# Gather passes of a graph kernel: one semaphore and one relay for eight gathers, and step addresses as two 16-bit words

## The chip, the cores and the metric

The kernel is one program on one core of a Trainium2 chip. The metric is the device time of one execution in microseconds (us), as the median of the runs; runs differ by some tenths of a per cent.

## The reference, cut to what matters

Four graph layers over N = 50000 nodes with 64 features and 50000 edges, each followed by a residual and mostly a layer norm. What matters here is the aggregation, which every layer has in some form: fetch a row for every edge by one index, and add it to the row of another index.

```python
edge_index = jnp.stack([src, dst])       # src random, dst sorted, 50000 * u**2
# layer 0
msgs = x[col] * norm[:, None]
out = jax.ops.segment_sum(msgs, row, num_segments=n)
# layer 1
transformed = xw[r, src]
out = jax.ops.segment_sum(transformed, dst, num_segments=num_node)
# layer 3, twice
return jax.ops.segment_sum(msg, dst, num_segments=n) + b
```

## The kernel before, in words

The program runs stage after stage, with a barrier between any two. It sorts the edges by source and by destination (each time 392 indirect DMAs write them to a list, L599), and then does four *stair passes* (`stair_pass`: e0, e1, e3, e4), an edge network (`mlp_pass`, which has a gather loop, two stair loops and semaphores of its own), and dense node passes in between (`node_pass`). Only the stair passes and the table that they read are touched.

**A stair pass.** The sorted edges lie in T = 392 tiles of 128; the nodes in 392 buckets of 128. Because edges are sorted, all pairs (tile, bucket) that share an edge form a stair, with STEPS = 784 steps, and each step either takes the next tile or the next bucket. A step is one product on TensorE: the one-hot matrix of the tile's destinations, times the 128 x 64 messages of the tile, added into the bucket's 64 columns of a ring in PSUM. Steps are done in GROUPS = 49 groups of GS = 16. The engines split the work so:

- GpSimd (POOL) issues one indirect DMA for each tile (L925), 392 in a pass, which gathers 128 rows into `msgs`, a ring of HELD = 128 tiles in SBUF. Gather i adds 16 to semaphore `slot{i % 8}` when it has landed, and gather i waits for gather i - 8 (L924). From tile 128 on, each batch of SLOTS = 8 gathers waits also for `s_room` (L922), that is, until the tiles that it overwrites have been used.
- SyncE (SP) relays. For each batch it waits for the group of TensorE that last uses the old tiles and adds 1 to `s_room` (L937 to L941), and then for each of the batch's eight tiles waits for its slot semaphore and adds 1 to `s_ready` (L943, L944). `s_ready` so counts the landed tiles in order.
- VectorE (DVE) makes the group's 16 one-hots with one instruction (L977), loads two words from `gates`, how many tiles and how many banks the group needs (L980, L981), waits until `s_ready` and `s_free` have reached them (L982, L983), and adds 1 to `s_go` (L985).
- TensorE (PE) loads the group's 16 step words from `table` into registers (L1046), waits for `s_go` (L1050), and does 16 matmuls (L1058). Both addresses of a step, the tile's column in `msgs` and the bucket's in the ring, lie packed in one 32-bit word, so each matmul has two register instructions ahead of it: REGISTER_ALU (in the trace ALU_OP) and ISA (in the trace FUSED_REGOPS). In the trace each f32 matmul is two MATMUL with two LDWEIGHTS.
- ScalarE (ACT) copies each full bank of the ring to `stage`, scaled in e3 and e4, and stores it (L1092 to L1131), and fills the bank with its starting rows.

What sets the order is therefore written out by hand; there is no scheduler. `Sorter.dve_table` (L438 to L495) makes `table`, `gates` and other tables on one partition; it runs twice, for the sources ahead of e0, and for the destinations inside e0, behind group 35. `mlp_pass` reads `table` of the sources as well and masks it for its own rings (L1367).

Of the kernel before, what the change touches and what calls it, by code (L numbers as in the profile page):

```python
# [10 lines left out]
I32 = mybir.dt.int32  # L11
# [234 lines left out]
class Sorter:  # L246
# [190 lines left out]
    def dve_table(self, dve):  # L437
# [23 lines left out]
        if "halves" in order:  # L461
# [5 lines left out]
            buckets = order["table"][:, :]  # L467
# [18 lines left out]
        nc.vector.tensor_scalar(gates[:, :, 1:2], rows_c[:, :, GS - 1:GS], 1.0, None, ALU.add)  # L486
        self.step(dve, nc.vector.tensor_copy(order["table"][:, :], self.steps_i[:, :]))
        self.step(dve, nc.vector.tensor_scalar(order["table"][:, :], order["table"][:, :], HELD - 1, None,
                                               ALU.bitwise_and))
        self.step(dve, nc.vector.tensor_scalar(order["table"][:, :], order["table"][:, :], 6, None,  # L490
                                               ALU.logical_shift_left))
        self.step(dve, nc.vector.tensor_scalar(self.within[:, :], self.within[:, :], 22, None,
                                               ALU.logical_shift_left))
        nc.vector.tensor_tensor(order["table"][:, :], self.within[:, :], order["table"][:, :], ALU.bitwise_or
                                ).then_inc(self.sem("steps"), 1)  # L495
# [338 lines left out]
def stair_pass(nc, label, K, order, column, source, sums, fresh=None, sort=None, extra=None, turned=None,  # L834
# [8 lines left out]
    with ExitStack() as ctx:  # L843
# [19 lines left out]
        s_land = K["slots_dma"]  # L863
        before = K["landed"]()
# [52 lines left out]
        def _(pool):  # L917
            if fresh is not None:
                pool.wait_ge(s_index, 1)
            for i in range(T):  # L920
                if i >= HELD and i % SLOTS == 0:
                    pool.wait_ge(s_room, (i - HELD) // SLOTS + 1)  # L922
                if i >= SLOTS:
                    pool.wait_ge(s_land[i % SLOTS], before + 16 * (i // SLOTS))  # L924
                pool.indirect_dma_start(  # L925
                    out=msgs[:, (i % HELD) * D:(i % HELD + 1) * D], out_offset=None, in_=source,
                    in_offset=bass.IndirectOffsetOnAxis(ap=order["index"][column][:, i:i + 1], axis=0)
                ).then_inc(s_land[i % SLOTS], 16)

        @block.sync  # L930
        def _(sp):
# [3 lines left out]
            for b in range(BATCHES):  # L935
# [5 lines left out]
                for i in range(b * SLOTS, (b + 1) * SLOTS):  # L941
                    sp.wait_ge(s_land[i % SLOTS], before + 16 * (i // SLOTS + 1))
                    sp.sem_inc(s_ready, 1)  # L943
# [76 lines left out]
        def _(pe):  # L1020
# [24 lines left out]
            for g in range(GROUPS):  # L1045
                _, at = nc.values_load_multi_w_load_instructions(  # L1046
                    order["table"][0:1, g * GS:(g + 1) * GS], [mybir.EngineType.PE], min_val=0,
                    max_val=((RING * BL - 1) * D << 16) + (HELD - 1) * D,
# [1234 lines left out]
def gnn(nc, x, src, dst, rel, ew, W, eW1, eb1, eW2, eb2, nW1, nb1, nW2, nb2, W1, b1, W2, b2, We, be, out):  # L2283
# [24 lines left out]
    with ExitStack() as ctx:  # L2308
        def sb(name, shape, dt=F32):
            return ctx.enter_context(nc.sbuf_tensor(name, shape, dt))  # L2310
# [120 lines left out]
```

## Time and profile before

| what | us |
|---|---|
| median of 3 runs | 5162.78 |
| lowest and highest of them | 5155.84, 5186.35 |
| span of the profiled execution | 6462.1 |
| stair passes in it (first gather to last matmul) | about 685, 657, 660, 660 |

The profile is of one execution with the hardware profiler on. The page gives its span and no further time of its own; the runs are timed without the profiler. The span is 1299 us, or 25%, above the median of the runs. Times of single instructions and the order of events are read from the profile; the length of a stretch has to be read with that difference in mind.

### The profile page before, as it was taken

How to read it: one execution, taken by the hardware profiler on the slowest of the kernel's cores; microseconds unless marked ns; L12 is line 12 of the kernel's file. 1: busy time of each engine (PE TensorE's matmuls, PEld its weight loads, DVE VectorE, ACT ScalarE, POOL GpSimd, SP SyncE). 2: the span in 40 equal slices, each digit the busy share in tenths (PEclk: the TensorE clock that was granted, in tenths of full speed). 3: DMA queues.
4: the chain of work that ended last, by engine and by line, in shares of the span. 5: the costliest groups of instructions: out<-in, count | busy, mean ns of one | idle time of the engine just before them, and what ended most of it. 6: DMA issues, size and time to landing. Idle time of an engine off the chain costs nothing. (4 is left out here: it accounts for less than half of the span.)

```text
span 6462.1 us, 74448 instructions
## 1 busy us (share of the span) xinstructions
PE 3919.6 (61%) x19983; PEld 3086.7 (48%) x19983; DVE 2177.2 (34%) x4653; ACT 1422.3 (22%) x3080; POOL 2886.1 (45%) x2799
## 2 busy tenths in 40 slices
PE   3333451668656742667466759888952669626697
PEld 2122121667422322666265646776732668426586
DVE  7444790324645620124311102343530112102134
ACT  0000000001333420112200126443420223302135
POOL 2555406663566766661555540000146660366602
PEclk8555575555666765555555569999975555755569
DMA  3000131111445641223734436554631222412235
GB/s 99 2 2 2 47 113 33 43 42 42 155 175 202 234 153 38 66 70 138 264 99 101 107 116 202 181 180 181 227 113 35 69 69 84 145 36 69 69 106 177
DMA packets 354959, 692.13 MB, mean 107 GB/s; under 512 B 183337, under 2 KB 185254, under 8 KB 339130
## 3 DMA queue, kind: packets, MB, share of 16 engines
q1 hardware_dynamic: 148381, 491.73, 21.7%
q10 hardware_dynamic: 118428, 130.12, 6.0%
q0 software_dynamic: 87808, 66.01, 5.8%
q8 instruction: 182, 2.98, 0.2%
q14 instruction: 160, 1.30, 0.1%
HBM read 350.87 MB, written 349.58 MB: 108 GB/s over the span
## 5 line engine op out<-in xcount | busy, mean ns | idle before, releaser
L1058 PE MATMUL e_ring<-e_msgs,e_hot 128*128 x6272 | 1419.4, 413 | 1091.3 <-issue 1082.7
L1058 PEld LDWEIGHTS e_ring<-e_msgs,e_hot 128*128 128x128 f32 x6272 | 1385.0, 328 | 1127.4 <-issue 1125.9
L925 POOL DMA_INDIRECT e_msgs<-y,index_D x784 | 741.4, 946 | 640.9 <-POOLq L77 261.1
L977 DVE TENSOR_TENSOR e_hot<-e_nodes,keys_D 128x2048 f32<-128x2048 f32 x147 | 336.9, 2292 | 1596.9 <-remote 872.0
L599 POOL DMA_INDIRECT list_D<-d_place,d_target x392 | 456.2, 1164 | 326.6 <-DVEq L553 210.5
L925 POOL DMA_INDIRECT e_msgs<-y,index_S x392 | 396.8, 1012 | 387.7 <-DVE index_S L963 198.3
L599 POOL DMA_INDIRECT list_S<-s_place,s_target x392 | 390.6, 996 | 362.8 <-DVEq L553 247.5
L1241 POOL DMA_INDIRECT m_far<-x,index_S x392 | 390.9, 997 | 347.9 <-DMA pairs_by_edge<-m_far 221.4
L1410 PE MATMUL m_ring<-m_region,m_hot 128*128 x1568 | 375.9, 426 | 215.7 <-issue 213.3
L925 POOL DMA_INDIRECT e_msgs<-x_by_relation,index_D x392 | 374.0, 954 | 210.4 <-issue 112.8
L1410 PEld LDWEIGHTS m_ring<-m_region,m_hot 128*128 128x128 f32 x1568 | 348.1, 328 | 244.3 <-issue 242.2
L2086 POOL TENSOR_TENSOR n_sq<-n_cent 128x1792 f32<-128x1792 f32 x14 | 44.4, 3175 | 837.0 <-DVE n_cent L1981 837.0
L1096 ACT ACTIVATE e_stage<-e_ring,dinv 128x64 f32<-128x64 f32 x784 | 171.6, 330 | 1078.5 <-DMA pairs_by_edge<-m_stage 475.6
L804 PE MATMUL s_p_deg<-s_hot_low,s_hot_high 128*128 128x392 f16 x784 | 256.0, 473 | 160.0 <-DVE s_hot_low L709 152.0
L1745 PE MATMUL d_p_w<-wall,d_xt 64*128 64x512 f32 x784 | 300.8, 808 | 80.9 <-DVE d_stage L1704 55.6
L1092 ACT COPY e_stage<-e_ring 128x512 f32<-128x512 f32 x98 | 57.4, 586 | 1211.1 <-remote 903.4
L2099 POOL TENSOR_TENSOR n_out<-n_cent,n_rstd 128x1792 f32<-128x1792 f32 x28 | 89.4, 3192 | 453.0 <-DVE n_rstd L1991 453.0
L1467 PE MATMUL m_ring<-m_region,m_hot 128*128 x1568 | 227.7, 303 | 59.6 <-issue 52.0
L1467 PEld LDWEIGHTS m_ring<-m_region,m_hot 128*128 128x128 f32 x1568 | 214.6, 190 | 72.7 <-issue 68.6
L1345 DVE TENSOR_SCALAR m_hot<-m_keyrow,slots 128x2048 f32<-128x2048 f16 x49 | 63.3, 1292 | 515.0 <-remote 280.1
L977 DVE TENSOR_TENSOR e_hot<-e_nodes,keys_S 128x2048 f32<-128x2048 f32 x49 | 112.2, 2290 | 341.9 <-remote 242.1
L522 DVE SCALAR_TENSOR_TENSOR s_scratch<-s_p_k,low_src,before 128x128 bf16<-128x128 f32 x392 | 113.6, 344 | 334.6 <-remote 303.4
(368 smaller groups left out, 5846.1 us busy)
## 6 DMA issues: line engine op xcount, KB each, us to landing
x_by_relation<-d_stage SPq DMA_DIRECT2D x98, 1024.0 KB
agg<-e_stage ACTq DMA_DIRECT2D x196, 256.0 KB
n_in<-agg SPq DMA_DIRECT2D x42, 896.0 KB, 5.6
x<-n_out SPq DMA_DIRECT2D x28, 896.0 KB, 3.6
m_keyrow<-keys_by_step SPq DMA_DIRECT2D x49, 512.0 KB
m_region<-pairs_by_edge SPq DMA_DIRECT2D x49, 512.0 KB
messages<-m_region SPq DMA_DIRECT2D x98, 256.0 KB
m_region<-messages SPq DMA_DIRECT2D x49, 512.0 KB, 4.1
```

The costliest lines, as they stand in the source:

```text
L522: op = self.nc.vector.scalar_tensor_tensor(out=self.scratch[:, h, j, :], in0=of[:, j, :], scalar=self.low[:, t:t + 1], in1=self.K["before" ...
L599: pool.indirect_dma_start(out=self.listing, out_offset=bass.IndirectOffsetOnAxis(ap=self.target[:, t:t + 1], axis=0), in_=self.place[:, t, ...
L804: mm = nc.tensor.matmul(p_deg[m // QUADS][:, 0:T], hot_high[m % 2][:, j, :], hot_low[m % 2][:, j, :], start=q == 0 and j == 0, stop=q == Q ...
L925: pool.indirect_dma_start(out=msgs[:, (i % HELD) * D:(i % HELD + 1) * D], out_offset=None, in_=source, in_offset=bass.IndirectOffsetOnAxis ...
L977: nc.vector.tensor_tensor(hot[g % 2][:, :, :], bc(nodes[:, 0:P].unsqueeze(1), [P, GS, P]), bc(order["keys"][:, g * GS:(g + 1) * GS].unsque ...
L1058: mm = nc.tensor.matmul(ring[:, bass.ds(bucket, D)], hot[g % 2][:, k, :], msgs[:, bass.ds(tile, D)], start=False, stop=False, skip_group_c ...
L1096: nc.scalar.activation(stage[r][:, k * D:(k + 1) * D], ring[:, at:at + D], ACT.Identity, scale=scale[:, m * BL + k:m * BL + k + 1]).then_i ...
L1241: pool.indirect_dma_start(out=far[:, (i % AHEAD) * D:(i % AHEAD + 1) * D], out_offset=None, in_=source, in_offset=bass.IndirectOffsetOnAxi ...
L1410: mm = nc.tensor.matmul(ring[:, bass.ds(tile, D)], hot[g % HOTS][:, k, :], region[:, bass.ds(bucket, D)], start=False, stop=False, skip_gr ...
L1467: mm = nc.tensor.matmul(ring[:, bass.ds(bucket, HID)], hot[g % HOTS][:, k, :], msgs[:, bass.ds(tile, HID)], start=False, stop=False, skip_ ...
L1745: nc.tensor.matmul(p_w[m % NW][:, :], xt[w % 2][half:half + D, k // 2, :], wall[half:half + D, :], start=True, stop=True).then_inc(s_pw, 1)
L2099: nc.gpsimd.tensor_tensor(result[0][h][:, :, :], cent[h][:, :, :], bc(rstd[h][:, :].unsqueeze(2), [P, CH, D]), ALU.mult).then_inc(s_done, 1)
```

## The change

In the stair passes the eight slot semaphores give way to two, `batch0` and `batch1`. All eight gathers of batch b add to `batch{b % 2}`; POOL waits once for each batch, for batch b - 2, and SP waits once for each batch and adds 8 to `s_ready` in one go. The sorts and the edge network keep the slot semaphores.

The table `table`, one 32-bit word for a step, becomes `pairs`, two 16-bit words for a step. PE loads 32 words for a group in place of 16. Other readers of the table view the pair as the same 32-bit word as before.

```diff
@@ dve_table
-        nc.vector.tensor_scalar(gates[:, :, 1:2], rows_c[:, :, GS - 1:GS], 1.0, None, ALU.add)
-        self.step(dve, nc.vector.tensor_copy(order["table"][:, :], self.steps_i[:, :]))
-        self.step(dve, nc.vector.tensor_scalar(order["table"][:, :], order["table"][:, :], HELD - 1, None,
-                                               ALU.bitwise_and))
-        self.step(dve, nc.vector.tensor_scalar(order["table"][:, :], order["table"][:, :], 6, None,
+        self.step(dve, nc.vector.tensor_scalar(gates[:, :, 1:2], rows_c[:, :, GS - 1:GS], 1.0, None, ALU.add))
+        pairs, tile = order["pairs"][:, :, :], self.clipped
+        self.step(dve, nc.vector.tensor_copy(tile[:, :], self.steps_i[:, :]))
+        self.step(dve, nc.vector.tensor_scalar(tile[:, :], tile[:, :], HELD - 1, None, ALU.bitwise_and))
+        self.step(dve, nc.vector.tensor_scalar(tile[:, :], tile[:, :], 6, None, ALU.logical_shift_left))
+        nc.vector.tensor_copy(pairs[:, :, 0], tile[:, :]).then_inc(self.sem("pre"), 1)
+        self.n += 1
+        self.step(dve, nc.vector.tensor_scalar(self.within[:, :], self.within[:, :], 6, None,
                                                ALU.logical_shift_left))
-        self.step(dve, nc.vector.tensor_scalar(self.within[:, :], self.within[:, :], 22, None,
-                                               ALU.logical_shift_left))
-        nc.vector.tensor_tensor(order["table"][:, :], self.within[:, :], order["table"][:, :], ALU.bitwise_or
-                                ).then_inc(self.sem("steps"), 1)
+        self.step(dve, nc.vector.tensor_copy(pairs[:, :, 1], self.within[:, :]))
+        nc.vector.sem_inc(self.sem("steps"), 1)
@@ stair_pass
-        s_land = K["slots_dma"]
-        before = K["landed"]()
+        s_batch = K["batch_dma"]
+        passed = next(K["stairs"])
+        before = [16 * SLOTS * ((BATCHES + 1 - r) // 2) * passed for r in range(2)]
@@ stair_pass, gpsimd
             for i in range(T):
+                b = i // SLOTS
                 if i >= HELD and i % SLOTS == 0:
                     pool.wait_ge(s_room, (i - HELD) // SLOTS + 1)
-                if i >= SLOTS:
-                    pool.wait_ge(s_land[i % SLOTS], before + 16 * (i // SLOTS))
+                if i % SLOTS == 0 and b >= 2:
+                    pool.wait_ge(s_batch[b % 2], before[b % 2] + 16 * SLOTS * (b // 2))
                 pool.indirect_dma_start(
...
-                ).then_inc(s_land[i % SLOTS], 16)
+                    in_offset=bass.IndirectOffsetOnAxis(ap=order["index"][column][:, i:i + 1], axis=0)).then_inc(s_batch[b % 2], 16)
@@ stair_pass, sync
-                for i in range(b * SLOTS, (b + 1) * SLOTS):
-                    sp.wait_ge(s_land[i % SLOTS], before + 16 * (i // SLOTS + 1))
-                    sp.sem_inc(s_ready, 1)
+                sp.wait_ge(s_batch[b % 2], before[b % 2] + 16 * SLOTS * (b // 2 + 1))
+                sp.sem_inc(s_ready, SLOTS)
@@ stair_pass, tensor
                 _, at = nc.values_load_multi_w_load_instructions(
-                    order["table"][0:1, g * GS:(g + 1) * GS], [mybir.EngineType.PE], min_val=0,
+                    order["pairs"][0:1, g * GS:(g + 1) * GS, :].rearrange("p s c -> p (s c)"), [mybir.EngineType.PE],
...
                     tile = nc.s_assert_within(
-                        at[k] & 0xffff, 0, (HELD - 1) * D,
+                        at[2 * k], 0, (HELD - 1) * D,
...
                     bucket = nc.s_assert_within(
-                        at[k] >> 16, 0, (RING * BL - 1) * D,
+                        at[2 * k + 1], 0, (RING * BL - 1) * D,
```

On PE, at the boundary between two groups of e0, the row order before was (`hot0` and `hot1` are the one-hots of even and odd groups):

```order
L1058 REGISTER_ALU
L1058 ISA
L1058 MATMUL e0_ring<-e0_msgs,e0_hot0 128x64
L1046 TENSOR_LOAD table_S
L1058 REGISTER_ALU
L1058 ISA
L1058 MATMUL e0_ring<-e0_msgs,e0_hot1 128x64
```

and at the same place it is now

```order
L1059 ISA
L1059 MATMUL e0_ring<-e0_msgs,e0_hot0 128x64
L1047 TENSOR_LOAD pairs_S
L1059 ISA
L1059 MATMUL e0_ring<-e0_msgs,e0_hot1 128x64
```

One register instruction of two is gone from each step (784 in a pass); the load stays one instruction at the same place, now of 32 words.

On POOL, the gathers of e0 from the first one on, with the semaphores that each waits for, before:

```order
L925 DMA e0_msgs<-y0,index_S0 128x64 [waits stair_index]
L925 DMA e0_msgs<-y0,index_S0 128x64 x7
L925 DMA e0_msgs<-y0,index_S0 128x64 [waits slot0]
L925 DMA e0_msgs<-y0,index_S0 128x64 [waits slot1]
L925 DMA e0_msgs<-y0,index_S0 128x64 [waits slot2]
...
L925 DMA e0_msgs<-y0,index_S0 128x64 [waits slot0,stair_room]
L925 DMA e0_msgs<-y0,index_S0 128x64 [waits slot1]
```

and now:

```order
L928 DMA e0_msgs<-y0,index_S0 128x64 [waits stair_index]
L928 DMA e0_msgs<-y0,index_S0 128x64 x15
L928 DMA e0_msgs<-y0,index_S0 128x64 [waits batch0]
L928 DMA e0_msgs<-y0,index_S0 128x64 x7
...
L928 DMA e0_msgs<-y0,index_S0 128x64 [waits batch0,stair_room]
L928 DMA e0_msgs<-y0,index_S0 128x64 x7
```

The gathers stand in the same order; of the 384 waits for a landing in a pass, 47 are left, each on the first gather of a batch.

## Rows read from the trace of the kernel before

**Rows 1.** The page, part 2: busy tenths, granted clock and DMA in 40 slices.

```profile
PE   3333451668656742667466759888952669626697
POOL 2555406663566766661555540000146660366602
PEclk8555575555666765555555569999975555755569
```

**Rows 2.** Stretches: gathers of e3, the rest of e3, gathers of e4, its rest.

```profile
core 0: us, PE busy (x) PEld busy (x) DVE busy (x) ACT busy (x) POOL busy (x), PEclk, DMA share, GB/s
4774.00:5335.00 561.00, 268.05 (x1121) 253.09 (x1121) 81.80 (x38) 78.28 (x299) 370.74 (x392) 0.50 0.23 57
5335.00:5440.00 105.00, 97.66 (x457) 97.29 (x456) 30.82 (x14) 36.15 (x144) 0.00 (x0) 0.50 0.20 66
5580.00:6140.00 560.00, 265.56 (x1117) 251.90 (x1118) 80.49 (x37) 77.03 (x292) 370.10 (x392) 0.50 0.22 57
6140.00:6246.00 106.00, 98.65 (x460) 98.09 (x460) 32.08 (x14) 37.41 (x149) 0.58 (x1) 0.50 0.20 66
```

**Rows 3.** Timeline of e3, POOL alone: gathers without (first eight) and with a wait.

```profile
4775.45 0.95 POOL L925 DMA_INDIRECT e_msgs<-y,index_D  x1 [0.30 <-issue]
...
4782.96 0.94 POOL L925 DMA_INDIRECT e_msgs<-y,index_D  x1 [0.30 <-issue]
4784.21 0.94 POOL L925 DMA_INDIRECT e_msgs<-y,index_D  x1 [0.30 <-issue]
...
4796.72 0.95 POOL L925 DMA_INDIRECT e_msgs<-y,index_D  x1 [0.30 <-issue]
```

**Rows 4.** Line L1058 (the steps) between 4860 and 4930 us of e3.

```profile
L1058 PEldq FUSED_REGOPS  x14: 84/84/700, 4859.6 to 4925.5; - x14
L1058 PEldq ALU_OP  x13: 32/32/691, 4861.0 to 4925.4; - x13
  issue: 125.5, 50
```

**Rows 5.** The same line between 5341 and 5434 us, behind the last gather of e3.

```profile
L1058 PE MATMUL e_ring<-e_msgs,e_hot x437: 421/421/421, 5340.6 to 5433.6; 128*128 x146
L1058 PEldq FUSED_REGOPS  x213: 80/84/84, 5340.9 to 5429.7; - x107
L1058 PEldq ALU_OP  x212: 32/32/32, 5341.1 to 5429.6; - x106
```

**Rows 6.** SP's relay (L943) between 4820 and 4930 us, and in the whole trace.

```profile
L943 SPq EVENT_SEMAPHORE  x79: 649/698/1396, 4820.4 to 4929.6; - x79
...
L943 SPq EVENT_SEMAPHORE  x1568: 4/17/1397, 957.4 to 6143.1; - x196
```

**Rows 7.** DVE's one-hots between 5335 and 5434 us: groups that PE paces.

```profile
L977 DVE TENSOR_TENSOR e_hot<-e_nodes,keys_D 128x2048 f32<-128x2048 f32 x14 | 32.1, 2292 | 63.4 <-PE e_ring L1058 56.9 <-remote 6.6
```

**Rows 8.** PE's load of 16 words (L1046) between 5341 and 5434 us.

```profile
L1046 PEldq TENSOR_LOAD <-table_D x13: 1102/1387/1395, 5342.1 to 5423.2; - x13
```

**Rows 9.** The edge network's second stair loop, at the full clock: PE's steps, and two boundaries.

```profile
4300.00:4380.00 80.00, 64.56 (x449) 60.78 (x448) 30.18 (x14) 32.92 (x56) 0.00 (x0) 1.00 0.49 159
...
4304.92 4.67 PE L1467 MATMUL m_ring<-m_region,m_hot 128*128 x32 [1.15 <-issue]
...
4310.61 1.61 PE L1467 MATMUL m_ring<-m_region,m_hot 128*128 x10 [1.03 <-issue]
```

**Rows 10.** DVE's table for the destinations, in e0: the steps that change.

```profile
1541.78 0.55 DVE L487 CAST table_D<-e_steps_i 1x784 int32<-1x784 f32 x1
...
1544.14 0.96 DVE L494 TENSOR_TENSOR table_D<-e_within,table_D 1x784 int32<-1x784 int32 x1
```

**Rows 11.** Waits on a semaphore at DVE (L985) and POOL (L924).

```profile
L985 DVEq EVENT_SEMAPHORE  x196: 49/50/50, 966.4 to 6228.8; - x196
...
L924 POOLq EVENT_SEMAPHORE  x132: 17/17/17, 1108.6 to 6121.0; - x132
```

More of the change, by code:

```diff
@@ L466, in dve_table @@
             self.n += 1
-            buckets = order["table"][:, :]
+            buckets = order["pairs"][0:1, :, :].rearrange("p s c -> p (s c)").bitcast(I32)
             self.step(dve, nc.vector.tensor_scalar(buckets, self.clipped[:, :], 22, None, ALU.logical_shift_left))
@@ L920, in _ @@
             for i in range(T):
+                b = i // SLOTS
                 if i >= HELD and i % SLOTS == 0:
                     pool.wait_ge(s_room, (i - HELD) // SLOTS + 1)
-                if i >= SLOTS:
-                    pool.wait_ge(s_land[i % SLOTS], before + 16 * (i // SLOTS))
+                if i % SLOTS == 0 and b >= 2:
+                    pool.wait_ge(s_batch[b % 2], before[b % 2] + 16 * SLOTS * (b // 2))
                 pool.indirect_dma_start(
                     out=msgs[:, (i % HELD) * D:(i % HELD + 1) * D], out_offset=None, in_=source,
-                    in_offset=bass.IndirectOffsetOnAxis(ap=order["index"][column][:, i:i + 1], axis=0)
-                ).then_inc(s_land[i % SLOTS], 16)
+                    in_offset=bass.IndirectOffsetOnAxis(ap=order["index"][column][:, i:i + 1], axis=0)).then_inc(s_batch[b % 2], 16)
         @block.sync
@@ L1046, in _ @@
                 _, at = nc.values_load_multi_w_load_instructions(
-                    order["table"][0:1, g * GS:(g + 1) * GS], [mybir.EngineType.PE], min_val=0,
-                    max_val=((RING * BL - 1) * D << 16) + (HELD - 1) * D,
+                    order["pairs"][0:1, g * GS:(g + 1) * GS, :].rearrange("p s c -> p (s c)"), [mybir.EngineType.PE],
+                    min_val=0, max_val=(HELD - 1) * D,
                     skip_runtime_bounds_check_because="both parts are masked to their rings before they are stored")
@@ L1365, in _ @@
                                         ).then_inc(s_b2, 1)
-            nc.vector.tensor_scalar(table, order["table"][:, :], (WHELD - 1) << 6 | (RING * QUAD - 1) << 22, None,
+            packed = order["pairs"][0:1, :, :].rearrange("p s c -> p (s c)").bitcast(I32)
+            nc.vector.tensor_scalar(table, packed, (WHELD - 1) << 6 | (RING * QUAD - 1) << 22, None,
                                     ALU.bitwise_and).then_inc(s_table, 1)
@@ L2325, in gnn @@
         K["slots_dma"] = [semaphore(f"slot{r}") for r in range(SLOTS)]
+        K["batch_dma"] = [semaphore(f"batch{r}") for r in range(2)]
+        K["stairs"] = itertools.count()
         passes = itertools.count()
@@ L2336, in gnn @@
                       "used": sb(f"used_{n}", [1, 64], U16), "keys": sb(f"keys_{n}", [P, STEPS]),
-                      "table": sb(f"table_{n}", [1, STEPS], I32), "gates": sb(f"gates_{n}", [1, GROUPS, 2], U16), "banks": sb(f"banks_{n}", [1, 64], U16)}
+                      "pairs": sb(f"pairs_{n}", [1, STEPS, 2], U16), "gates": sb(f"gates_{n}", [1, GROUPS, 2], U16), "banks": sb(f"banks_{n}", [1, 64], U16)}
                   for n, columns in (("S", (0, 2)), ("D", (0, 2)))}
```

## Prediction

> **What bounds the kernel now.** I read four views. First the slices of the page [rows 1]: POOL is busy six or seven tenths through each stair pass and never more, PE about as much, and the clock granted to PE there is 0.5, the 1.2 GHz level. No engine is full. Second the stretches of e3 and e4 [rows 2]: 392 gathers are 561 us long though POOL is busy for only 371 of them, and then PE works alone for 99 us more. So in the profile the gathers are held up, and the pass is 660 us long. Third the timeline of POOL at the start of a pass [rows 3], where nothing holds it: a gather is 0.95 us and the next begins 0.30 us later, 1.25 us in all, 392 x 1.25 = 490 us a pass. Fourth, who holds the gathers up in the profile: PE, and PE is held by nothing of the program. Between 4860 and 4930 us a register addition, which takes 32 ns [rows 5], lasts up to 691 ns, and PE idles 125.5 us (both of its rows together) "on issue" [rows 4]; at the same time SP's semaphore steps last 698 ns against 17 in the median [rows 6]. Behind the last gather both are calm again: 457 half-matmuls take 97.6 us [rows 2], 0.2136 us each, 32 x 0.2136 = 6.84 us a group. DVE's one-hots, made one for each group that PE finishes, say the same: (32.1 + 63.4) / 14 = 6.82 [rows 7].
>
> An addition on registers touches no memory. That it takes twenty times as long while the profiler writes a record for each instruction of PE and SP I read as the profiler's own cost. It fits the other number: the span is 1299 us above the median of the runs. Taken at the gathers' pace a stair pass would be 490 us and a tail of some 10, 500 in place of 660, some 160 less in each of four passes, 640 in all; that is half of the 1299, and the edge network's first loop, which packs its steps in the same way, can hold more of it. So the picture I argue from is: without the profiler each stair pass goes at POOL's pace, 1.25 us a gather; PE needs 6.84 us a group, 49 groups or 335 us, and waits for tiles; and the end of the pass is the last gather's landing plus what PE has to do behind it.
>
> Everything below is in microseconds added to the median of the runs, 5162.8, and not to the span, since the span carries the profiler's share. The measurement tells from no change what is above about 1%, some 52 us.
>
> **The change part by part.**
>
> *POOL's waits.* In each pass 384 waits become 47: 337 fewer, 1348 in four passes. What is one worth? The first eight gathers of a pass have no such wait, and the ninth and later ones have: starts 4775.45 to 4782.96 are 7.51 us for six gathers, and 4784.21 to 4796.72 are 12.51 for ten [rows 3], 1.25 both times. A wait that is satisfied costs nothing on top. Bounds: below, nothing (a wait removed can't cost); above, the whole gap of 0.30 us that stands ahead of each gather, 1348 x 0.30 = 404 us. I take 0, since both kinds of gather stand side by side in the trace. The new wait, for batch b - 2 at the first gather of batch b, asks for a gather nine back where it was eight, so it holds nothing up; queued behind it are only the next gathers.
>
> *PE's register instruction.* It is gone 784 times a pass, 32 ns each [rows 5]: 25 us a pass of PE's sequencer. Cover: the array needs 0.427 us a step (2 x 0.2136) and the two register instructions 0.116, and in the gathers' pace PE waits for tiles anyway. Bounds 0 and 4 x 25 = 100 us less; I take 0, because behind the last gather, where PE does set the pace, matmuls follow each other with no gap while both register instructions are there [rows 2, 5].
>
> *PE's load of 32 words.* 16 words take 1.39 us [rows 8]. At the low clock they are hidden by matmuls queued earlier; in the edge network's second loop, at the full clock (1.00), a load of 16 words shows as a gap of 1.03 to 1.15 us at each group [rows 9]. If the price goes by the word, 32 take 2.78, or 1.39 more. Against that stand 16 x 0.032 = 0.51 of additions removed. Bounds: 0, and 196 groups x 0.88 = 172 us more. I take 0: the load comes ahead of the wait for `s_go`, and at the gathers' pace PE has 10 - 6.84 = 3.2 us to spare in a group of eight tiles; at the end of a pass the group's 16 steps need 16 x 0.116 + 2.78 = 4.6 us of the sequencer against 6.84 of the array.
>
> *SP's relay: the term that counts.* `s_ready` rises by eight when the eighth tile of a batch is in. A group that needs one tile of a batch now waits for all eight. In mid-pass this is a shift without a price: PE comes up to 7 x 1.25 = 8.75 us later and the ring of 128 tiles (160 us) has room for it. At the end it isn't. I counted from the reference's indices how many tiles the last groups need: by source, groups 46, 47 and 48 need 377, 385 and 392; by destination 381, 387 and 392. Before, by source, group 47 could start when tile 385 was in, seven gathers or 8.75 us ahead of the last, and was done (6.84) when the last landed; the pass ended 6.84 us behind the last landing. Now group 47 waits for the last batch, and both groups stand behind it: 13.68. That is 6.8 us more. By destination the 387 tiles were in 6.25 us ahead, so 6.84 + 0.6 before, and 13.7 now, 6.3 more; group 46 and those ahead of it are late as well by the same rounding, which brings it to about 7. Four passes: 4 x 6.8 = 27 us. Bounds: at the full clock a group is half as long and the term 14 us; if the tail were hidden, 0. I take 27, since all four passes show 0.50 [rows 1, 2], and a loop of the same steps ran for 99 us without a pause and stayed there.
>
> *DVE's table.* Removed is one `or` of 0.96, added are two copies of 0.55 [rows 10]: +0.14 us, twice; once inside e0, where DVE waits for tiles anyway, once ahead of it. The copies write 16-bit words at a stride; if that doubled them it would be 1.1 us more each time. I take 0.
>
> Sum: 0 + 0 + 0 + 27 + 0 = +27 us, 5162.8 + 27 = 5190, 0.5% slower and so within what counts as no change.
>
> **The rivals.**
>
> *A: the waits cost something that the trace hides.* The gap of 0.30 us is read with the profiler on. If a third of it were the wait, 0.10 us, 1348 would give 135 us back: 5190 - 135 = 5055. For it: the kernel's time hangs on POOL's pace over 1568 gathers. Against it: equal pitch with and without [rows 3], and where DVE and POOL do show a wait as an instruction of its own it takes 50 and 17 ns [rows 11]; at 50 the gain is 67, 5123, still no change. The Trainium skill (Advanced Engine Details and Errata, Network/Comms) gives 50 to 100 ns for reading a semaphore from a sequencer; by that, an estimate from the page's figure, 1348 waits would be 67 to 135 us and the time 5055 to 5123. The trace doesn't agree as far as the pitch goes, since nothing is added by it there.
>
> *B: the slow stretches are real.* Then the timed passes, too, are 660 and not 500 us, and PE and SP are slow at each small instruction while gathers run. One of two register instructions is gone and seven of eight relays, so about half the excess goes: 4 x 160 / 2 = 320, 5190 - 320 = 4870. Against it: there is no place left for the 1299 us between span and median.
>
> *C, slower: the load of 32 words sets the pace.* Place: the boundary of two groups on PE. Price: 0.88 us a group net, in 49 x 4 groups 172, so 5190 + 172 = 5362. It decides once the array's queue holds less than the load, that is, when PE and not POOL paces the pass and the clock is at its full level, as in rows 9. Against it: 0.50 in all four passes. Between this and my case lies one in which only the destination passes' later half is paced by PE, +27 + 74 x 0.88 = +92, 5255.
>
> *D: the tail is hidden or shorter,* because PE in the unprofiled run is at the full clock: 5163 to 5177.
>
> **How the numbers follow.** My case 0.55, D 0.13, A 0.13, B 0.07, C with its milder form 0.12. Faster by over 1% (under 5111): A and B, 0.20. Slower by over 1% (over 5214): C, 0.12. The rest, 0.68, within 1%. The range holds my case, D, the near half of A and the lower edge of C: 5085 to 5225; outside it are B, the far half of A and most of C, about 0.2.
>
> **What would show each step right or wrong.** The profiled span should fall by far more than the time: half the records of the slow stretches are gone, so e3 should be nearer 580 than 660 us with the time unmoved. If the time falls with it, B is right. The pitch of gathers should stay 1.25 us; 1.15 or less means A. The last two groups of each pass should both begin behind the relay of the last batch, where the gathers pace the pass. Loads of 32 words should last about 2.8 us with the matmuls behind the last gather still 6.84 us a group; gaps there mean C. I am wrong if the median is outside 5085 to 5225, and wrong in the reason if it is inside while the pitch of the gathers has moved.

## The result, and the profile after

The changed kernel takes 5438.64 us in the median of four runs (5433.59 to 5457.4), the kernel before 5173.91 in four runs of its own (5155.84 to 5186.35). The ratio is 1.0512, with a 95% interval of 1.0474 to 1.0551: 265 us slower. I had forecast 5190, with 5225 as the upper end of the range.

One thing has to be said of the chips. The kernel before takes 5174 us where the result was measured and 5181 on the chip of runs e8, e9 and e10 (the first kind below), and 6451, 6510 and 6515 us on three others (the second kind). Its first profile, with a span of 6462 us, looks like one of the second kind; on which chip it was taken is not on record. Every ratio of the experiments is taken on one chip, and every run says what the kernel before took there.

The page after, part 2, the same three rows as [rows 1]:

```profile
PE   4656566666784266654998797789756668666677
...
POOL 2777677735777677724777500001177740577602
PEclk9775655557888555555556899999855556655579
```

The clock of the stair passes is 0.5 as before. POOL is now seven tenths busy in a pass, where it was six; that is the chip and not the change, for in a pass of run e8, the kernel before but for one bound, POOL is busy for 370 of 489 us, here for 370 of 495. Four stretches, in the order of [rows 2]: the gathers of pass e3, its rest, the gathers of pass e4, its rest.

```profile
core 0: us, PE busy (x) PEld busy (x) DVE busy (x) ACT busy (x) POOL busy (x), PEclk, DMA share, GB/s
3951.30:4446.10 494.80, 308.10 (x1370) 296.21 (x1371) 101.00 (x45) 98.06 (x373) 369.82 (x392) 0.50 0.28 74
4446.10:4516.10 70.00, 45.75 (x208) 44.46 (x207) 11.46 (x5) 14.70 (x61) 0.91 (x1) 0.50 0.08 28
4669.40:5164.70 495.30, 308.17 (x1374) 296.78 (x1374) 101.01 (x45) 98.06 (x373) 369.81 (x392) 0.50 0.28 74
5164.70:5233.90 69.20, 45.02 (x204) 43.73 (x203) 11.46 (x5) 14.62 (x61) 0.91 (x1) 0.50 0.08 28
```

The gathers take 495 us, as I had worked out for passes without the slow stretches (490). But PE ends 70 us behind them and not 10, and it isn't busy in that time: 45.75 of 70. What it does instead is in the timeline of PE, and in the rows of its load and of its steps:

```profile
4386.27 7.08 PE L1059 MATMUL e_ring<-e_msgs,e_hot 128*128 x32 [4.14 <-issue]
4397.48 7.08 PE L1059 MATMUL e_ring<-e_msgs,e_hot 128*128 x32 [4.12 <-issue]
```

```profile
L1047 PEldq TENSOR_LOAD <-pairs_D x147: 7526/7945/8307, 1863.9 to 5218.7; - x147
L1047 PEldq TENSOR_LOAD <-pairs_S x49: 7684/7932/10655, 642.8 to 1228.5; - x49
...
L1059 PEldq FUSED_REGOPS  x3136: 55/55/65, 650.9 to 5229.4; - x196
...
  issue: 1683.6, 384
  DVEq L986: 61.8, 8
```

The load of 32 words lasts 7.9 us, where 16 words took 1.1 to 1.39 [rows 8]. It stands on PE's sequencer in the middle of a group's boundary. One of them, seen with the array at the same place:

```profile
L1047 PEldq TENSOR_LOAD <-pairs_D x2: 7938/7956/7974, 4142.8 to 4154.0; - x2
```

```profile
4154.60 3.41 PE L1059 MATMUL e_ring<-e_msgs,e_hot 128*128 x15
4162.13 7.08 PE L1059 MATMUL e_ring<-e_msgs,e_hot 128*128 x32 [4.12 <-issue]
```

The sequencer begins the load at 4154.0, when it has issued the last step of a group; the array still works off what is queued until 4158.01. So 4.0 us of the load are hidden and 4.1 us show, at each boundary. A group is 7.08 + 4.12 = 11.2 us long, 49 of them are 549, and the pass is 565 us (3951.3 to 4516.0). The gathers deliver a group's eight tiles in 10 us, so PE has become the slower one: in the 196 groups of the four passes it waits for DVE's go 8 times. The one-hots say it from DVE's side: in the 14 groups of [rows 7] 56.9 of DVE's 63.4 us of idle time ended on PE, and here, over three whole passes, 1162.6 of 1288.6.

```profile
L978 DVE TENSOR_TENSOR e_hot<-e_nodes,keys_D 128x2048 f32<-128x2048 f32 x147 | 336.9, 2292 | 1288.6 <-PE e_ring L1059 1162.6
```

SP's relay is 17 ns in all 196 cases, in [rows 6] up to 1397 (run e6, the same kernel on a chip of the second kind, has 17 ns in all 196 as well):

```profile
L944 SPq EVENT_SEMAPHORE  x196: 17/17/17, 650.8 to 5168.2; - x196
```

### The profile page after: what moved, and what is told of

It reads as the page before. It is cut to its first block and busy times, and to the rows that moved or that the text cites. A ratio compares the mean times of both kernels' runs of the same rounds, so it can differ in the third digit from the quotient of the medians.

```text
span 5455.3 us, 69944 instructions
## 1 busy us (share of the span) xinstructions
PE 3736.5 (68%) x19983; PEld 3005.4 (55%) x19983; DVE 2175.4 (40%) x4655; ACT 1416.3 (26%) x3080; POOL 2913.6 (53%) x2799
## 5 line engine op out<-in xcount | busy, mean ns | idle before, releaser
L1059 PE MATMUL e_ring<-e_msgs,e_hot 128*128 x6272 | 1388.4, 423 | 853.8 <-issue 792.0
L1059 PEld LDWEIGHTS e_ring<-e_msgs,e_hot 128*128 128x128 f32 x6272 | 1352.6, 332 | 891.6 <-issue 891.6
L978 DVE TENSOR_TENSOR e_hot<-e_nodes,keys_D 128x2048 f32<-128x2048 f32 x147 | 336.9, 2292 | 1288.6 <-PE e_ring L1059 1162.6
L600 POOL DMA_INDIRECT list_S<-s_place,s_target x392 | 407.6, 1040 | 212.7 <-issue 118.8
L1242 POOL DMA_INDIRECT m_far<-x,index_S x392 | 405.8, 1035 | 130.5 <-issue 114.0
L805 PE MATMUL s_p_deg<-s_hot_low,s_hot_high 128*128 128x392 f16 x784 | 244.1, 455 | 179.9 <-DVE s_hot_low L710 179.7
L1412 PE MATMUL m_ring<-m_region,m_hot 128*128 x1568 | 342.2, 422 | 23.3 <-DVEq L1358 20.5
L1412 PEld LDWEIGHTS m_ring<-m_region,m_hot 128*128 128x128 f32 x1568 | 337.7, 332 | 28.4 <-issue 26.6
L1747 PE MATMUL d_p_w<-wall,d_xt 64*128 64x512 f32 x784 | 227.3, 701 | 78.5 <-DVE d_stage L1706 75.9
L1469 PE MATMUL m_ring<-m_region,m_hot 128*128 x1568 | 224.4, 301 | 65.8 <-issue 55.5
L1469 PEld LDWEIGHTS m_ring<-m_region,m_hot 128*128 128x128 f32 x1568 | 213.1, 189 | 77.2 <-issue 74.8
L805 PEld LDWEIGHTS s_p_deg<-s_hot_low,s_hot_high 128*128 128x128 f16 x784 | 76.2, 119 | 305.8 <-DVE s_hot_low L710 250.0
L1774 ACT COPY d_stage<-d_p_w 128x512 f32<-128x512 f32 x294 | 160.8, 589 | 168.4 <-PE d_p_w L1747 161.1
```

The costliest lines, as they stand in the source:

```text
L600: pool.indirect_dma_start(out=self.listing, out_offset=bass.IndirectOffsetOnAxis(ap=self.target[:, t:t + 1], axis=0), in_=self.place[:, t, ...
L805: mm = nc.tensor.matmul(p_deg[m // QUADS][:, 0:T], hot_high[m % 2][:, j, :], hot_low[m % 2][:, j, :], start=q == 0 and j == 0, stop=q == Q ...
L978: nc.vector.tensor_tensor(hot[g % 2][:, :, :], bc(nodes[:, 0:P].unsqueeze(1), [P, GS, P]), bc(order["keys"][:, g * GS:(g + 1) * GS].unsque ...
L1059: mm = nc.tensor.matmul(ring[:, bass.ds(bucket, D)], hot[g % 2][:, k, :], msgs[:, bass.ds(tile, D)], start=False, stop=False, skip_group_c ...
L1242: pool.indirect_dma_start(out=far[:, (i % AHEAD) * D:(i % AHEAD + 1) * D], out_offset=None, in_=source, in_offset=bass.IndirectOffsetOnAxi ...
L1412: mm = nc.tensor.matmul(ring[:, bass.ds(tile, D)], hot[g % HOTS][:, k, :], region[:, bass.ds(bucket, D)], start=False, stop=False, skip_gr ...
```

## The experiments

The runs are called e0 to e13 after their labels; the stair passes have names of the same form, so here it is always run e3 or pass e3. Two theories. The load: words of 16 bits cost 0.25 us each on their way into a register, and the 4 us that this puts above what is hidden make nearly all of the 265. The relay: coarse steps of `s_ready` let PE begin late, and the batches cost more than the 27 us that I gave them. Beside them the question whether the slow stretches of the first profile [rows 4, 6] belong to the profiler or to the chip.

### The kernel before again, and each part alone

Run e0 is the kernel before, unchanged. Run e1 keeps the packed table and takes the semaphores and the relay of the change; run e2 keeps slots and relay and takes the pairs:

```diff
@@ e1: only this of the change
-                if i >= SLOTS:
-                    pool.wait_ge(s_land[i % SLOTS], before + 16 * (i // SLOTS))
+                if i % SLOTS == 0 and b >= 2:
+                    pool.wait_ge(s_batch[b % 2], before[b % 2] + 16 * SLOTS * (b // 2))
...
+                sp.wait_ge(s_batch[b % 2], before[b % 2] + 16 * SLOTS * (b // 2 + 1))
+                sp.sem_inc(s_ready, SLOTS)
@@ e2: only this of the change
-                    order["table"][0:1, g * GS:(g + 1) * GS], [mybir.EngineType.PE], min_val=0,
+                    order["pairs"][0:1, g * GS:(g + 1) * GS, :].rearrange("p s c -> p (s c)"), [mybir.EngineType.PE],
```

> The kernel before, unchanged, with its profile taken again. Its first profile spanned 6462 us while its runs took 5174, whereas the changed kernel's profiled span and time agree (5455 and 5457). If the slow stretches of PE and SP (1.4 us from one small instruction to the next) are the recorder's, they and a span of about 6460 should come again with a time near 5174, and the ordinary time leaves 5174 / 5439 as it is. If the first profile was a disturbed execution, the span should now be near 5174, gathers paced at 1.25 us, and each stair pass about 500 us.

> The kernel before with the two batch semaphores and one relay for eight tiles, step words still packed in 32 bits. Theory (the load of 32 words is the whole loss): 5174 plus what the coarser relay costs at the end of each pass, 0 to 27 us, so 5174 to 5201, with loads of 16 words at 1.4 us or less. Rival (the coarse relay and the batch wait hold the passes up): most of the 265 us is here, 5400 or more.

> The changed kernel with the eight slot semaphores and a relay for each tile put back; step words stay pairs of 16 bits. Theory: PE paces each pass at 11.2 us a group (a load of 8.0 us that the queued matmuls cover only in part), so the relay doesn't matter: 5430 to 5440, loads of 32 words at 8.0 us. Rival (coarse relay): back near 5174.

On this chip the kernel before takes 6450.68 us in the median. Run e0: 6454.78, with a span of 6452.7. Neither of the two cases that I had named came: the time itself is 6455. Span and time of the same execution are 2 us apart, so the long passes are in the timed runs too, and they are not the profiler's. Run e1: 6441.4, ratio 0.9999 (0.9973 to 1.0025), nothing. Run e2: 6701.87, ratio 1.0389 (1.0337 to 1.0441), 251 us. Of the two parts only the pairs cost time here, and their load is as long as in the changed kernel:

```profile
L1046 PEldq TENSOR_LOAD <-pairs_D x147: 7517/7892/8481, 2432.6 to 6468.8; - x147
```

On this chip the loss sits in another place of the pass than on the first kind. Pass e3, its gathers and its rest, in run e0 and then in run e2:

```profile
4785.80:5345.20 559.40, 269.20 (x1125) 253.82 (x1126) 82.71 (x38) 79.16 (x301) 368.88 (x391) 0.50 0.23 57
5345.20:5443.40 98.20, 96.88 (x453) 96.39 (x452) 29.79 (x13) 33.24 (x132) 0.94 (x1) 0.50 0.21 67
```

```profile
4916.20:5473.30 557.10, 253.22 (x1096) 243.32 (x1096) 82.70 (x38) 79.16 (x301) 368.85 (x391) 0.50 0.24 58
5473.30:5636.50 163.20, 106.23 (x480) 103.53 (x480) 29.79 (x13) 33.23 (x132) 0.94 (x1) 0.50 0.12 40
```

The gathers take as long as before; the 65 us are all behind the last gather, where 14 or 15 groups are still to do, at 11.1 us each in place of 6.84. On the first kind it is 49 groups that take 11.2 us where the gathers would have let them take 10. Both come to some 60 us a pass; nothing in the traces ties the two numbers to each other.

### What of the load costs: its words, their number or their width

Run e3 is the whole change, with the pairs of the destinations as 32-bit words; those of the sources stay 16-bit. (It uses an existing buffer for the edge network's blank tile, to make room, and so does run e9 below.) Run e4 loads the 32 words with two instructions of 16. Run e7 loads only the 16 words of 8 steps for a group and uses them twice. Run e5 is run e1 again and run e6 the changed kernel again, on the chip of run e4 and run e7.

```diff
@@ e3, against the changed kernel
-                      "pairs": sb(f"pairs_{n}", [1, STEPS, 2], U16)
+                      "pairs": sb(f"pairs_{n}", [1, STEPS, 2], U16 if n == "S" else I32)
@@ e4, against the changed kernel
-                    order["pairs"][0:1, g * GS:(g + 1) * GS, :].rearrange("p s c -> p (s c)"), [mybir.EngineType.PE],
+                for half in range(2):
+                    part = slice(g * GS + half * HS, g * GS + (half + 1) * HS)
+                    _, some = nc.values_load_multi_w_load_instructions(
+                        order["pairs"][0:1, part, :].rearrange("p s c -> p (s c)"), [mybir.EngineType.PE],
...
+                    at += list(some)
@@ e7, against the changed kernel
-                    order["pairs"][0:1, g * GS:(g + 1) * GS, :].rearrange("p s c -> p (s c)"), [mybir.EngineType.PE],
+                    order["pairs"][0:1, g * GS:g * GS + HS, :].rearrange("p s c -> p (s c)"), [mybir.EngineType.PE],
...
-                        at[2 * k], 0, (HELD - 1) * D,
+                        at[2 * (k % HS)], 0, (HELD - 1) * D,
```

> The changed kernel with the destinations' pairs as two 32-bit words for a step (the sources' pairs stay 16-bit; the edge network uses an old buffer for its zeros to make room). 32 words are still loaded by one instruction. Theory W (the width sets the price: 16-bit words are fetched one by one, 0.25 us each): the loads of e1, e3 and e4 fall to about 2.8 us, these passes to about 505 us, and the time by 3 x 60 us to about 5260; e0 keeps loads of 8 us. Rival C (more than 16 words is what costs): loads stay at 8 us everywhere and the time at 5439.

> The changed kernel with its load of 32 16-bit words for a group cut into two loads of 16 words. Theory W (each 16-bit word is fetched by itself, 0.25 us): two loads of 4.0 us, the time as in the changed kernel, 4 to 5% above the kernel before. Rival C (one load of more than 16 words is what costs): two loads of 1.4 us and a time within 1% of the kernel before.

> The kernel before with the batch semaphores and one relay alone, once more, to see the relay's own price. Where the kernel before takes about 5174 (gathers pace its passes) theory says 0 to 27 us more, ratio 1.000 to 1.005, with the last two groups of each pass behind the last landing; where it takes about 6450 (PE paces the passes and lags the gathers by 100 us) the relay can't show: ratio 1.000, as e1 had.

> The changed kernel, unchanged, beside the others. On a chip where the kernel before takes about 5174 it should take 5440 (ratio 1.051); on one where that takes about 6450 it should take what e2 took, 6700 (ratio 1.039), since the batch semaphores cost nothing there by e1.

> The changed kernel with only the first eight steps' words of a group loaded (16 words of 16 bits) and used again for the other eight steps, so half of the sums are of the wrong tiles and buckets; the number of matmuls and register instructions stays. Theory: a load of 4.0 us, a group of PE at about 4.0 + 3.2 = 7.2 us, below the 10 us of eight gathers; the passes go back to the gathers' pace and the time to that of the kernel before plus the relay's 0 to 27 us, where that takes 5174. Rival (something else in the pairs, not the load, costs): the time stays at the changed kernel's.

Run e3 ran on the chip of run e1: 6516.53, ratio 1.0103 (1.0057 to 1.015). One kernel has both widths in it, with the same count of 32 words:

```profile
L1047 PEldq TENSOR_LOAD <-pairs_D x147: 2127/2422/3031, 2400.8 to 6256.8; - x147
L1047 PEldq TENSOR_LOAD <-pairs_S x49: 7521/7912/10587, 956.3 to 1699.4; - x49
```

That is 0.08 us a word for 32 bits, and 0.25 for 16. The three passes with 32-bit words are back to the length of the kernel before (pass e3: 654.6 us against 657.6 in run e0), and the one pass that still has the long load, pass e0, is 762 us against 688. That is 74 us more there, and 67 more in the four passes together, where the time is 66 above the kernel before.

On the next chip the kernel before takes 6509.95. Run e4: 6777.13, ratio 1.0397 (1.0363 to 1.0432); run e6, the changed kernel: 6751.92, ratio 1.0376 (1.0341 to 1.0411). Two loads cost about as much as one, 2 x 3.8 = 7.6 us: the price hangs on the words, not on the instruction. Run e7: 6497.8, ratio 0.9992 (0.9972 to 1.0013). With half the words the load lasts 3.8 us, just under the 4.0 us of queued matmuls that hide it, and by the median the whole loss of 242 us is gone, not half of it. (In the profiles some of it stays in pass e0, 707 us in run e7 against 686 in run e5, and why is open; the other three passes agree to about 1 us.) Run e5: 6501.52, ratio 0.9986 (0.997 to 1.0003).

```profile
L1050 PEldq TENSOR_LOAD <-pairs_D x294: 3781/3796/4502, 2448.2 to 6548.8; - x147
```

```profile
L1047 PEldq TENSOR_LOAD <-pairs_D x147: 3782/3796/4703, 2379.7 to 6265.9; - x147
```

The first of the two is run e4, the second run e7.

### The relay where gathers set the pace, one register instruction, and the run-ahead

Run e10 is run e1 once more. Run e9 keeps slots, relay and the packed sources, and gives the destinations two 32-bit words for a step, with one register instruction. Run e8 is the kernel before with gathers at most 64 tiles ahead.

```diff
@@ e9, against the kernel before
-                        at[k] & 0xffff, 0, (HELD - 1) * D,
+                        tiles[k] if tiles else at[k] & 0xffff, 0, (HELD - 1) * D,
...
-                      "table": sb(f"table_{n}", [1, STEPS], I32)
+                      **({"table": sb(f"table_{n}", [1, STEPS], I32)} if n == "S" else {"pairs": sb(f"pairs_{n}", [1, STEPS, 2], I32)})
@@ e8, against the kernel before
-                if i >= HELD and i % SLOTS == 0:
-                    pool.wait_ge(s_room, (i - HELD) // SLOTS + 1)
+                if i >= WHELD and i % SLOTS == 0:
+                    pool.wait_ge(s_room, (i - WHELD) // SLOTS + 1)
```

> The batch semaphores and the one relay for eight gathers, with the packed 32-bit table as before, once more. Where the kernel before takes about 5174 us, its passes go at the gathers' pace of 1.25 us, and my term for the relay (both last groups stand behind the last batch) is 4 x 6.8 = +27 us, ratio 1.005, bounds 0 and 27. The rival is that POOL's 1348 waits do cost something (0.10 us each would be -135 us, ratio 0.974). Where the kernel before takes about 6450 to 6510 us, PE's slow groups set the pace and both theories say a ratio of 0.999 to 1.001.

> The slot semaphores of before; the destinations' addresses (three of four stair passes) as two 32-bit words with one register instruction for a step, the sources' packed as before. The load of 32 words should last 2.4 us. If the instruction saved is worth what its record says (3 x 784 x 0.032 = 75 us) and PE's sequencer sets the pace, ratio 0.985 to 0.99; if the array sets it and the load's 1.0 us more is hidden behind queued matmuls, ratio 1.000; if the load's extra is not hidden, 147 x (1.03 - 0.51) = 76 us more, ratio 1.012.

> The kernel before, with the gathers allowed only 64 tiles ahead of the steps, not 128. Theory: the slow stretches of PE and SP (register instructions of 0.7 us where they last 0.03) come from gathers that run far ahead, and end when the gathers are held; then half the run-ahead makes them shorter and the time falls, ratio below 0.98 where the kernel before takes about 6450 to 6510 us. Rival: they have nothing to do with how far ahead the gathers are; ratio 0.998 to 1.01, since PE sets the pace and 64 tiles are still 80 us of cover.

This chip is of the first kind: the kernel before takes 5181.0 us. Run e10: 5210.65, ratio 1.0057 (1.0026 to 1.0088), so the relay and its batches cost 30 us (13 to 46). Run e9: 5185.93, ratio 0.9988 (0.9955 to 1.0021): the register instruction saved on three passes, and 1.0 us more of load, show nothing either way (the interval is 17 us to each side). Run e8: 5190.54, ratio 1.0028 (0.9995 to 1.0061).

In this profile of run e8 PE has no slow stretch, so the theory of the run-ahead was not put to the test. It is the kernel before but for the run-ahead, so it also shows what [rows 2] could not: a pass at the gathers' pace. (Run e9, with 128 tiles of run-ahead, has pass e3 at 499 us; the unchanged kernel before was never profiled on such a chip.) Pass e3 in run e8, then in run e10, gathers and rest:

```profile
3804.80:4293.80 489.00, 345.19 (x1544) 333.30 (x1544) 112.43 (x50) 110.91 (x425) 369.79 (x391) 0.51 0.30 79
4293.80:4304.80 11.00, 7.08 (x32) 6.90 (x32) 0.00 (x0) 1.75 (x8) 0.95 (x1) 0.50 0.13 30
```

```profile
3838.40:4331.70 493.30, 339.53 (x1513) 327.06 (x1514) 110.19 (x49) 108.90 (x417) 368.91 (x391) 0.50 0.29 77
4331.70:4345.40 13.70, 13.66 (x65) 13.47 (x64) 2.29 (x1) 3.50 (x17) 0.94 (x1) 0.50 0.15 43
```

500.0 us against 507.0. Of the 7 only 2.7 are in the tail. The ends of PE, run e8 ahead of run e10:

```profile
4286.68 7.09 PE L1058 MATMUL e_ring<-e_msgs,e_hot 128*128 x32 [1.73 <-DVEq L985]
4297.72 7.08 PE L1058 MATMUL e_ring<-e_msgs,e_hot 128*128 x32 [3.95 <-DVEq L985]
```

```profile
4314.50 7.08 PE L1059 MATMUL e_ring<-e_msgs,e_hot 128*128 x32 [2.76 <-DVEq L986]
4324.62 20.74 PE L1059 MATMUL e_ring<-e_msgs,e_hot 128*128 x96 [3.03 <-DVEq L986]
```

In run e8 group 47 begins at 4286.68, 7.1 us ahead of the start of the last gather, and the last group waits 3.95 us for its tiles. In run e10 groups 46, 47 and 48 stand in a row of 20.74 us: 46 waited for the batch that ends with the 384th tile, and the other two queue behind it. The rest of the 7 us is in the gathers, at three places 112 gathers apart:

```profile
3976.98 0.94 POOL L927 DMA_INDIRECT e_msgs<-y,index_D  x1 [0.30 <-issue]
3978.22 0.94 POOL L927 DMA_INDIRECT e_msgs<-y,index_D  x1 [0.30 <-issue]
3981.25 0.94 POOL L927 DMA_INDIRECT e_msgs<-y,index_D  x1 [2.08 <-issue]
```

The gather after the 113th of a pass (and the 225th and the 337th) comes 3.0 us behind the one ahead of it in place of 1.25: 3 x 1.75 = 5.3 us a pass, in the passes e1, e3 and e4 of run e10 alike, and at the same gathers of the changed kernel. In run e8 and run e9, with a wait on each gather, no gather of these passes is more than 1.5 us behind the last. POOL waited for nothing that the profile shows; why it stalls is not known.

### A last look: pairs alone, half the load, the kernel before

> Slot semaphores as before, pairs of 16-bit words. Where the kernel before takes about 5174 us: the result's +265 less the relay's 30 of e10 is 235, ratio 1.045, with the loads at 7.9 us and PE setting the pace at 11.2 us a group, 49 groups in about 550 us. Rival: the two parts only hurt together (PE comes late because the relay is late), then less than 1.03. Where the kernel before takes about 6450 us: 1.039 as in e2.

> The changed kernel with only the 16 words of 8 steps loaded for a group and used twice (half of the sums go to wrong tiles and buckets). The load lasts 3.8 us, shorter than the 4.0 us by which the sequencer runs ahead of the array, so PE keeps 6.9 to 7.1 us a group, the gathers set the pace, and what stays is the relay: ratio 1.003 to 1.009. Rival: each microsecond of load counts, then half of the 235 us, ratio about 1.028.

> The kernel before. Where it takes about 5174 us, its passes e3 and e4 should be about 500 us from first gather to last matmul (392 gathers at 1.25 us and a tail of some 10), with no register instruction of 0.7 us, and the span within 10 us of the time; the 660 us of the first profile would then be that of another chip, and not the recorder's work. Rival: passes of 660 us under the profiler and a span some 1300 us above the time.

The code is that of run e2, run e7 and run e0. I had hoped for a chip of the first kind, and this one is of the second: the kernel before takes 6514.67. Run e11: 6771.46, ratio 1.0409 (1.0354 to 1.0463). Run e12: 6511.58, ratio 1.0002 (0.9979 to 1.0025). Run e13: 6502.53, with a span of 6500.5. They repeat run e2, run e7 and run e0 on another chip of the second kind and say nothing on the first kind. Pass e3 of run e13, its gathers and its rest, is that of [rows 2] again, with span and time 2 us apart:

```profile
4817.70:5381.30 563.60, 265.73 (x1114) 251.92 (x1114) 80.40 (x37) 76.82 (x292) 368.92 (x392) 0.50 0.22 57
5381.30:5482.60 101.30, 99.40 (x464) 98.86 (x463) 32.08 (x14) 35.58 (x142) 0.90 (x1) 0.50 0.20 66
```

### Where the 265 us come from

The four passes e0, e1, e3 and e4 of the changed kernel, first gather to last matmul, are 604, 565, 565 and 564 us long. In run e10, which lacks only the pairs, they are 529, 511, 507 and 507; in run e8 they are 524, 504, 500 and 500. So from run e8 to run e10 it is 25 us, from run e10 to the changed kernel 245, together 270, against 265 measured. Of the 25, some 17 are in the gathers and 7 in the tails. The split on the chips of the first kind rests on these lengths and on run e10's ratio; neither the pairs alone nor half a load was ever run on one.

## Why the prediction was wrong, point by point

**The step that failed is the term for PE's load of 32 words.** I took 0 with 172 us as the upper bound and gave the slower case a chance of 0.12; by the lengths of the passes it is 245 us. The mechanism was the one that I named in rival C, the load at the boundary of two groups. Its size was off: I priced 32 words from 16 words of another width, 2.78 us where 7.9 were measured. I knew that the words became 16-bit and still went by their number. The rows that would have warned me were in the trace of before, where single 16-bit words are loaded, on DVE and on SP:

```profile
L980 DVEq TENSOR_LOAD <-gates_D x147: 281/285/439, 2357.8 to 6226.4; - x147
```

```profile
L1332 SPq TENSOR_LOAD <-used_S x41: 248/256/472, 4109.8 to 4344.2; - x41
```

32 x 0.25 is 8.0 us. They warn, and don't prove: a load of one word can't tell a price per word from a price per load. Against it stood 16 words of 32 bits in 1.39, 0.087 a word. A bound from the nearest rows had to take both. With the 4.0 us that the trace after shows hidden (no row of before gives it), its upper end would have been 8.0 - 4.0 = 4.0 us a group on PE alone. With 49 groups of 11.1 against the gathers' 490 us a pass, that is 544 against 490, some 216 us in four passes and a time of about 5380, or about 5400 with the relay's 27. The Trainium skill (Runtime: NRT & Kernel Launch, Instruction fetch mechanics) gives about 200 ns for each register of a TENSOR_LOAD, even in bulk; by that 32 words would be, as an estimate, 6.4 us. The page speaks of loads that the runtime adds, and not of a kernel's own. The 16-bit words agree nearly, with 0.25 us; the 32-bit blocks, 0.07 to 0.09 us a word, do not.

**The condition of C was wrong too.** I wrote that it decides only "when PE and not POOL paces the pass and the clock is at its full level". At the half clock the array's queue covers 4.0 us of load, and the gathers' slack another 2.9 (10.0 - 7.08); 7.9 us are more than both, and all four passes were paced by PE at 0.50. Run e7 shows the first part from below, on the second kind of chip: behind the last gather 3.8 us of load leave a group at 7.0 us and the time where it was. (The sum beside it, 16 x 0.116 + 2.78 = 4.6 us, still held the register instruction that the change removes; without it it is 4.1. It changes nothing.)

**SP's relay: the sum was right, the working was not.** +27 was taken, and run e10 measured 30 (13 to 46). But group 47 needs 384 tiles, not 387 or 385: in run e8 it gets its go with the 384th relay in pass e3, and in pass e0, by source, too. So the tail grows by 2 to 3 us in each of the passes e1, e3 and e4 and not at all in pass e0 (11.4 us from the last gather to the end in run e8, 11.1 in run e10), 7 us in all and not 27. The other 17 are in the gathers, where POOL stalls; I had not foreseen that. That the two add up to nearly my number is chance.

**POOL's waits: 0, right for the pitch.** It is 1.25 us with and without them, in the changed kernel too (3951.3 to 4446.1 is 494.8 for 391 gathers, of which 5.3 are the stalls: 1.252). Rival A is out. But the stalls came with the batches, and if they belong to the waits that are gone, this term is +17 and not 0; no run separates the two. (L985, the DVE row of [rows 11], is the step that adds to `s_go`, so its 50 ns are not the price of a wait alone.)

**PE's register instruction: 0, right.** Run e9 gives 0.9988 (0.9955 to 1.0021). Beside it, FUSED_REGOPS fell from 84 to 55 ns, and nothing came of that.

**DVE's table: 0.** No run tells it apart, and none needs it.

**The reading of the profile was half wrong.** That the timed passes are some 500 us long held for the chips that gave the times (500.0 in run e8). That the long passes were "the profiler's own cost" did not: run e0 and run e13 have them with span and time 2 us apart. On the chips where they occur rival B is right that they are real, and wrong on what makes them long. With seven of eight relays gone (run e1, run e5) the ratio is 0.9999 and 0.9986, and with one of two register instructions gone as well (run e12) it is 1.0002. More than that: in run e2, run e6, run e7, run e11 and run e12 no register instruction of these steps lasts more than 65 ns, in run e7 no relay more than 17, and the passes are as long as before or longer. In the same stretch of the pass PE still starts its half-matmuls one by one, 7 or 8 in 20 us, while POOL goes on at 16 gathers in 20 us; the second row is 80 us later, behind the first pause of the gathers:

```profile
4942.00:4962.00 20.00, 1.98 (x8) 2.02 (x7) 0.00 (x0) 0.00 (x0) 15.11 (x16) 0.50 0.13 26
5022.00:5042.00 20.00, 13.95 (x63) 14.09 (x64) 4.58 (x2) 4.68 (x18) 13.21 (x14) 0.50 0.26 74
```

So PE's matmuls come late there with no long register instruction beside them: those of [rows 4] are one sign of the slow stretch and not its cause.

**One sign misled.** I had written that pass e3 should be nearer 580 than 660 us. It is 565, but by chance: this is a chip of the first kind, where the pass takes 500 us in run e8. The sign that told was another, gaps between groups behind the last gather, and it came as rival C has it.

## What to carry to other kernels

Price a load into registers by the width of its words, from a row of the same width: here 16-bit words cost 0.24 to 0.25 us each, and 32-bit words in a block 0.07 to 0.09. For these 16 steps, one block of packed 32-bit words and a 32 ns register instruction a step are 1.1 + 0.5 us of the sequencer, two 16-bit words a step 7.9. Two 32-bit words a step are 2.1, and run e9 shows no difference in time to the packed ones. At the half clock a load on TensorE's sequencer was hidden up to the 4.0 us of matmuls queued ahead of it, and what was longer stood open at each group; so 3.8 us cost next to nothing and 7.9 us some 60 us a pass. What an open gap costs depends on what else paces the pass. And where the span of a profile and the median of the runs differ, compare the time of the profiled execution itself before putting the difference down to the profiler.

## What had not been expected of the hardware

- The cost of 16-bit words in a TENSOR_LOAD on PE: 16 words 3.80 us, 32 words 7.9, two loads of 16 twice 3.80. That is by width at the same count in one kernel (run e3). What in the engine makes it so is not known. For 32-bit words it is 1.1 us for 16 and 2.13 (run e9) to 2.42 (run e3) for 32.

```profile
L1059 PEldq TENSOR_LOAD <-pairs_D x147: 2127/2132/2150, 1810.9 to 4944.9; - x147
```

- The same program takes 5174 to 5181 us on some chips and 6451 to 6515 on others. Each chip with a number on record was used on one occasion only, so a property of the chip and one of the occasion can't be told apart. On the second kind PE starts its work late in a stretch early in each pass, while gathers run, as shown above for run e7. In the kernel before, register instructions of PE and SP's semaphore steps last up to 1.4 us there (L943 in run e13, below), and on the first kind they don't (run e8, the second row). What causes it is open: taking these instructions away did not shorten the time (run e1, run e12), and run e8, which was meant to test whether the gathers' run-ahead causes it, met a chip where the stretches don't occur.

```profile
L943 SPq EVENT_SEMAPHORE  x1568: 3/17/1412, 964.7 to 6178.0; - x196
```

```profile
L943 SPq EVENT_SEMAPHORE  x1568: 17/17/17, 642.3 to 4936.3; - x196
```

- POOL's three stalls of 1.75 us, 112 gathers apart, which appear when most gathers carry no wait (run e10 and the changed kernel) and not when all do (run e8, run e9). Open as well.
